# Sparse experts on one core: TensorE makes the down calls of a slot before it transposes the next slot's product

## The reference

```
logits = einsum('th,eh->te', x, router_w);  top_vals, top_idx = top_k(logits, 2)
expert, weight = top_idx[:, 0], softmax(top_vals)[:, 0]
gate = einsum('th,eih->eti', x, gate_w);  up = einsum('th,eih->eti', x, up_w)
act  = silu(gate) * up
out  = the expert's act @ down_w[expert].T * weight
x    = x + tanh(g_ffn[0]) * out
```

## Time and profile before

| what | value |
|---|---|
| median of 3 runs | 375.36 us (374.71 to 375.99) |
| profiled execution, whole time | 376.61 us |
| its span, first to last instruction | 374.8 us |
| TensorE busy, its weight loads | 337.2 us (90%), 211.1 us (56%) |
| DVE, ACT, POOL busy | 241.2 us (64%), 161.3 us (43%), 101.9 us (27%) |
| mean granted clock of TensorE | 0.968 |
| the slots' steps | from 88.4 us to 129.0 us of the span |

### The profile page before, as it was taken

How to read it: one execution, slowest core, us unless ns; L and a number is a source line. 1 busy time by engine, 2 the same in 40 slices (tenths; PEclk the granted TensorE clock), 3 DMA queues, 4 the chain that set the end, 5 groups by cost and what they waited for, 6 DMA issues and landing times.

```text
span 374.8 us, 4935 instructions
## 1 busy us (share of the span) xinstructions
PE 337.2 (90%) x1581; PEld 211.1 (56%) x1590; DVE 241.2 (64%) x564; ACT 161.3 (43%) x333; POOL 101.9 (27%) x154
## 2 busy tenths in 40 slices
PE   2999886498999998999899999989899889999997
PEld 1494666386888745555545645643534444445885
DVE  4358884873545549899948984982433458778911
ACT  2433472434333223147766666875863233333000
POOL 7302664460000275502341234432550001000000
PEclk9999998559999989999999999999999999999999
DMA  7998000026111214600000000000000000000011
GB/s 207 374 422 241 1 16 2 28 84 212 43 46 56 71 56 138 256 0 9 0 9 0 1 2 7 3 0 9 0 0 3 0 0 0 0 2 0 29 44 42
DMA packets 14026, 22.57 MB, mean 60 GB/s; under 512 B 2049, under 2 KB 11393, under 8 KB 13186
## 3 DMA queue, kind: packets, MB, share of 16 engines
q1 hardware_dynamic: 13234, 20.16, 15.7%
q0 software_dynamic: 768, 2.10, 1.8%
HBM read 15.96 MB, written 6.03 MB: 59 GB/s over the span
## 4 chain that ended last, share of the span: by engine, by line
PE 65%; DVE 19%; ACT 6%; issue 4%; POOL 2%; DMA 2%; SPq 1%; DVEq 0%; ACTq 0%; POOLq 0%
PE bank L260 46%; DVE mx L1302 6%; PE bank L480 5%; PE bank L448 4%; PE bank L379 3%; ACT region L978 3%; DVE stats L1048 2%; PE bank L451 2%; PE bank L276 2%; PE bank L270 2%; ACT s_high L938 1%; DVE x_sb L1088 1%; DMA x_sb<-in_x_dram 1%; POOL rstd L751 1%; PE bank L495 1%
## 5 line engine op out<-in xcount | busy, mean ns | idle before, releaser
L978 ACT ACTIVATE region<-bank,padcol 128x512 f32<-128x512 f32 x96 | 62.4, 695 | 18.1 <-PE bank L260 17.3
L1302 DVE TENSOR_REDUCE mx<-bank 128x2 f32<-128x512 f32 (+1 forms) x96 | 61.0, 685 | 9.9 <-remote 4.9
L260 PE MATMUL bank<-xT,e_gu 128*128 128x512 f32 x128 | 57.6, 594 | 0.5 <-ACT xT L832 0.5
L815 POOL TENSOR_SCALAR_AFFINE_SELECT region<-region 128x1024 f32<-128x1024 f32 x32 | 35.0, 1094 | 81.5 <-ACT region L978 81.4
L260 PE MATMUL bank<-qst,kblk 128*128 128x512 f32 x96 | 46.0, 489 | 0.8 <-DMA qst<-nmT 0.3
L448 PE MATMUL bank<-kblk,qst 128*128 128x512 f32 x96 | 43.5, 470 | 1.5 <-DVE mx L1302 1.1
L260 PEld LDWEIGHTS bank<-xT,e_gu 128*128 128x128 f32 x128 | 23.3, 190 | 25.1 <-issue 24.3
L747 POOL TENSOR_SCALAR veps<-mv 128x1 f32<-128x1 f32 x40 | 11.2, 279 | 63.6 <-DVE mv L1050 63.6
L451 PE MATMUL bank<-causb,identb 128*128 128x256 bf16 (+1 forms) x90 | 28.3, 314 | 0.0
L260 PE MATMUL bank<-e_down,region 128*128 128x256 f32 x128 | 27.8, 379 | 0.0
L1088 DVE SCALAR_TENSOR_TENSOR x_sb<-bank,tg,x_sb 128x256 f32<-128x256 f32 x24 | 11.6, 484 | 25.0 <-PE bank L260 24.9
(11 more groups left out here) (179 smaller groups left out, 644.2 us busy)
## 6 DMA issues: line engine op xcount, KB each, us to landing
e_gu<-in_e_gu_dram SPq DMA_DIRECT2D x2, 1408.0 KB, 12.2
x_sorted<-zero SPq DMA_DIRECT2D x1, 1920.0 KB, 9.4
y_sorted<-region SPq DMA_DIRECT2D x15, 128.0 KB, 1.7
x_sb<-in_x_dram SPq DMA_DIRECT2D x4, 256.0 KB, 4.4
ctxT<-in_ctxT_dram SPq DMA_DIRECT2D x2, 512.0 KB, 6.7
e_down<-in_e_down_dram SPq DMA_DIRECT2D x1, 1024.0 KB, 14.4
region<-x_sorted SPq DMA_DIRECT2D x1, 1024.0 KB, 7.5
e_gu<-in_f_gate_dram SPq DMA_DIRECT2D x1, 1024.0 KB, 4.8
```

The lines of the kernel that those rows point to most:

```text
L260: return pe.matmul(dst, lhsT, rhs, start=first, stop=last)
L815: pool.affine_select(out=block, in_=block, compare_op=ALU.is_ge, fill=0.0, base=0, pattern=[[0, 2], [0, PER_GROUP], [1, P]], channel_multi ...
L978: taken(act.activation(dst, src.rearrange("p (h n) -> p h n", n=SEQ - mt * P), ACT.Exp, bias=padcol[:, key:key + 1], scale=float(HD) ** -0 ...
L1302: taken(dve.reduce_max(mx[:, b % 2, nt, quads, q, hg], src, AX), "sa")
```

## The change

In every step of the slots' loop TensorE's items 3 and 4 change places: down of slot i-1 comes before the product turn of slot i. No call is added or taken away, and no other engine's order changes.

```diff
                 if i + 2 < SLOTS:
                     slot_turn(i + 2)
-                if i < SLOTS:
-                    slot_act_turn(i)
                 if i == 1:
                     pe.wait_ge(sem("down_split"), 4)
                 if i >= 1:
                     slot_down(i - 1, expert[i - 1])
+                if i < SLOTS:
+                    slot_act_turn(i)
```

## The result

| | median | runs | ratio to before, 95% interval |
|---|---|---|---|
| before | 375.68 us | 374.71 to 376.45 (4) | |
| after | 383.85 us | 383.69 to 385.55 (4) | 1.0224 [1.0197, 1.0251] |

The change costs 8.2 us. The forecast was 380.0 (377.2 to 382.0): the direction is right, the size is nearly twice the forecast, and the range does not hold it. The profiled execution took 383.69 us.

The account below looks back on a forecast made before the run. The x loop was taken to set the step, with TensorE alone on the chain behind the slots. The median 375.36 us plus 4.6 us for the later last down, with zero clock change, gave 380.0 us, range 377.2 to 382.0.

Parts of the forecast that it names:

- The x loop: In the slots before the change, x turn, ACT, DVE, gate and up set the step of 2.638 us.
- the loop of the downs: In the changed slots, down, product turn, ACT's pieces, DVE's low pieces, next down form a loop setting the step, 2.79 us.
- Its length: Loop of the downs per step: 2.79 us, the rows' 2.82 less a little, 0.15 us above the step of before.
- the allowance for a turn that might have waited: The rows' 2.82 us was lowered to 2.79 because the product turn at 126.24 may have waited for its product.
- The term of 4.6 us: Down of slot 14 starts 4.6 us later: about 2.5 us from the tail, 2.1 us from the longer steps.
- Half the clock behind the slots: Behind the slots, the half-clock stretch that cost 1.8 us comes again, perhaps earlier; entered as zero change.
- the rival of 0.12: Idle time before the last two downs brings a half-clock stretch lasting twice as long: 381.8 us, chance 0.12.
- What follows passes the shift on, but for 0.4 us: Behind the last down, at least the shift less 0.4 us, which DVE could give back, goes through to the end.
- TensorE issuing ahead: Rival in the slots: the product turn covers TensorE's issue work, steps fall to 2.38 us, time 374.3 us; chance 0.04.

## Why the prediction was wrong, point by point

- *The x loop sets the step before.* Right: with the x turn ahead the step fell to 2.46 us.
- *The change closes the loop of the downs.* Right: two slots' distance opens it again (2.64 us), and the x turn ahead does nothing for it.
- *Its length.* 2.79 us forecast, 2.83 measured in 12 of the 14 distances; the sum of the rows of before, 2.82, was the better number, and the allowance for a turn that might have waited was not needed. The first distance was longer, 3.01 us, for a reason that is not shown, and the last, at half clock, 3.86.
- *The term of 4.6 us.* Somewhat small. With the waits filled and the clock at 1.00, the last down came 132.85 - 87.94 = 44.9 us after the first gate and up, 5.3 later than before: 0.04 in each step and 0.2 in the first distance were missing. The time of that kernel, 380.66 - 375.78 = 4.9 us above before, is near the forecast and within its range. By parts, the middle steps cost 2.3 us where 2.1 were forecast.
- *Half the clock behind the slots, "zero change".* This is the step that failed. Between the changed kernel and the same with the waits filled lie 383.85 - 380.66 = 3.2 us (4.0 by the two profiles, counted from the first gate and up); with the waits empty the time lies outside the range, with the waits filled inside. The prediction named the cause (idle time of more than a microsecond in front of the last downs) and saw that a stretch "may begin earlier", but entered it as nothing, and priced the rival of 0.12 as a second stretch of the length of before, in the filler alone. The stretch was four times as long and also covered a down, a product turn, the last down and the key calls: 1.03 us in the distance of the last two downs, 1.58 in the ten calls behind. The argument against it was that step 0 idles for a microsecond without a fall. That is so (1.00 from 86 to 95 us of before), but it is one wait with whole gate and up calls on both sides; in the changed tail two such waits stand with one down and one turn between them. Which of these differences counts is not shown.
- *What follows passes the shift on, but for 0.4 us.* Right where the clock stayed up: with the waits filled, the last down came 5.3 us later and the end 5.0 (291.4 against 286.4 us from the first gate and up), and TensorE came to wait for the queries, as foreseen. One reading was a little off: on TensorE's timeline of before the transposes began at 139.36 and not 139.52, so the filler had 0.7 us to give and not 0.8; nothing hangs on it.
- *TensorE issuing ahead.* It fell: the 0.24 or 0.25 us between DVE's piece and the down is there in every step from the second on, and the product turn came 0.20 or 0.21 us behind the last down call wherever the changed kernel's clock was 1.00, as rows 6 and 7 had it.

## What to carry to other kernels

When two pieces of an in-order engine's work change places, follow each of them round to its next wait: the piece that now stands behind a wait closes a loop through other engines, and the length of that loop, to be read where the old trace happens to run it alone, is the new step. A pipeline's last steps, where no other work fills such a loop, pay its whole length, and if they leave TensorE idle, the clock is a term of the sum with the calls of the tail in it, not only those behind. The cheap ways out are one more step of distance, which brought the step back to 2.64 us here (though not the whole time, which stayed 2.1 us above before), or issuing the awaited piece earlier; the latter, on the other loop, made the kernel of before 2.4 us faster.

## What the runs showed of the hardware that was not expected

- In the changed kernel the clock fell within the first of two waits of 1.30 us (before 128.40, the wait ends at 128.61) and stayed at half for 13.5 us; with only the last steps changed it fell within the second (at 128.9, the wait ends at 129.59), for 10.2 us; with ten filler calls in these waits it did not fall.
- Such waits are not the only way to it. With no wait above 0.4 us in the last steps, the half clock behind the slots lasted 3.4 us in the kernel before, 7.0 us in the kernel before with the x turn ahead and in the kernel with the down two slots behind, and was absent in the profile with changed order only in the middle. What makes these differ is open.
- The clock came back late: in the changed kernel 5.5 us after the filler began (136.4 to 141.9), although TensorE had worked without a gap from 132.47 on; in the kernel before 3.3 us after the filler began (130.56 to 133.9).
- In the same code ahead of the slots the half clock lasted 17.1 us in one profile and 20.5 us in another. The slots then began 1.9 us apart.
